# A graph network kernel on one core: one chunk's convolution a step later, a weight product in another bank, a re-ordered tail

## The chip, the core and the metric

The kernel runs on one core of one Trainium2 chip. That core has a matrix engine (TensorE, PE in the rows below, with PEld for its weight loads), a vector engine (VectorE, DVE), a scalar engine (ScalarE, ACT), GpSimd (POOL), a queue engine that only issues transfers here (SyncE, SP) and 16 DMA engines. The engines run side by side and wait for each other by semaphores. The metric is device microseconds (us) of one launch. Three runs of the kernel before gave 517.07, 517.53 and 518.02 us; the median is 517.53 us.

## The reference

The input is a batch of 16 graphs of 512 nodes with 128 features, `x`, and dense adjacency matrices `adj` of 512 x 512. Two networks follow one another, each with a residual sum and a layer norm:

```python
# 1: gated graph network, 5 layers, on every graph
A = (adj != 0)
h = x
for l in range(5):
    m   = einsum('bnd,de->bne', h, weight[l])
    agg = einsum('bij,bid->bjd', A, m)
    gi, gh = agg @ w_ih.T + b_ih, h @ w_hh.T + b_hh      # three gates each
    r, z = sigmoid(i_r + h_r), sigmoid(i_z + h_z)
    h = (1 - z) * tanh(i_n + r * h_n) + z * h
x = layernorm(x + h * nodemask)

# 2: group convolutions on nodes 0..24 of every graph, 5 groups of nodes
for g, idx in enumerate(GROUPS):
    N_g = D^-1/2 (adj[idx, idx] + I) D^-1/2
    h1  = relu(N_g @ (x[idx] @ W1[g]) + b1[g])           # 128 -> 256
    o   = relu(N_g @ (h1 @ W2[g]) + b2[g])               # 256 -> 128
    fused[idx] += softmax(fusion_w)[g] * o
out = layernorm(x + fused)
```

Everything is float32 on the outside.

## The kernel before

**Recurrence.** A step is one layer of one graph; 16 graphs and 5 layers give `K` = 80 steps, in the fixed order `GRAPH` (made from the table `ROUNDS`). A state lies transposed (feature on the partition) in float32 (`H`) and as two float16 halves (`HT`, high and low). In step k the matrix engine does, in this order: `aggregate(k + 1)`, 8 matmuls of the *next* step's messages with the adjacency matrix (fp8) into one of two banks `pA2`; `gates_of_state(k)`, three float16 products each into `pHN`, `pR` and `pZ`; `gates_of_messages(k)`, three each added into `pR` and `pZ` and written into `pIN`. The products into `pIN` wait for `h_v` = k, the end of step k-1's new state, because the engines work out the new state inside `pIN`. ScalarE reads the gates through sigmoid and tanh and makes the high halves (`aggregated_hi`, `state_hi`, `reset_gate`, `update_gate`, `new_gate`); VectorE does the low halves, the candidate and the new state (`aggregated_lo`, `candidate`, `new_state`, `state_lo`); GpSimd multiplies z and h (`kept_share`). A state goes back to node order for `aggregate` by a transposing transfer that SyncE issues two steps ahead.

**First layer norm.** After a graph's last step, `masked` (times the mask), `residual` (GpSimd), `stats_of_rows` and `variances` (VectorE), `inverse_root` (GpSimd), `scales` (VectorE: the shift `NB` for ScalarE, and for the first 32 nodes the normalised rows `X1`, semaphore `f_nb`) and `normalise` (ScalarE) follow, some steps apart; then SyncE stores the graph (`store_y`). Graphs 10 and later come back through `back`, four matrix transposes.

**Convolution.** Nodes 0 to 31 of four graphs make one chunk, four chunks in all. A chunk passes through seven stages on the matrix engine, all through the bank `pC`: A (`conv_a`: X1 with the normalised adjacency `BD`), B twice (`conv_b`: W1, one half of the 256 each), S twice (`conv_s`: W2), D twice (`conv_d`: `BD` again). ScalarE reads A, B and S, VectorE adds the biases and reads D, and `fused` sums the groups with a ReLU. The table `CONV_AT` says in which step each stage of chunks 0 to 2 is put, with 0 for "ahead of the aggregation" and 1 for "between the gates". `conv_a(c)` waits for `f_nb` = 4(c + 1), the scales of the chunk's four graphs. Graph 7, the last of the second chunk, has its last step at 47 and its `scales` on VectorE in step 53.

**Start and tail.** Before step 0 the weights are transposed and `merge(0)` multiplies layer 0's weight with the input gates' weights into `pA2[:, 1]`, where VectorE has just read the other weights (`wh_lo`). In the last two steps (78 and 79) the last chunk is worked out early in small tiles (`early_...`, tile `X` from `pA`), and after step 79 its stages B, S and D run in the banks of `LAST_BANKS`, beside the layer norms of graphs 12 to 15. S and D are split there as group 0 and groups 1 to 4. The biases are put into the bank first by a product with the identity (`biases`).

The order of every engine's work is the order of the code of its block; there is no scheduler. Each engine waits at the head of its own queue.

Of the kernel before, what the change touches and what calls it, by code (L numbers as in the profile page):

```python
# [6 lines left out]
ALU = mybir.AluOpType  # L7
# [8 lines left out]
B, N, D = 16, 512, 128  # L16
L = 5
NI = N // P
K = B * L
# [60 lines left out]
           [(54, 0), (55, 0), (56, 0), (57, 0), (58, 0), (60, 0), (61, 1)],  # L80
# [34 lines left out]
def graph_net_kernel(nc, x, adj, nodemask, weight, w_ih, w_hh, b_ih, b_hh, W1, b1, W2, b2, fusion_w, out):  # L115
    ctx = ExitStack()
    with ctx:
# [113 lines left out]
        LAST_BANKS = [pA2[:, 1, :], pC, pA2[:, 0, :], pA2[:, 1, :], pC, pA2[:, 0, :], pC]  # L231
# [79 lines left out]
        f_dn = sem("f_dn")  # L311

# [29 lines left out]
        def _(sp):  # L342
# [36 lines left out]
            def store_y(b):  # L379
                sp.wait_ge(f_on, b + 1)  # L380
                if b == B - 1:
                    sp.wait_ge(f_dn, 1)
# [46 lines left out]
        def _(pool):  # L429
# [191 lines left out]
        def _(pe):  # L621
# [206 lines left out]
            pe.wait_ge(wi_v, 1)  # L828
            pe.wait_ge(wh_lo, 1)
            merge(0, pA2[:, 1, :])  # L830
# [4 lines left out]
            pe.wait_ge(wc_lo, 1)  # L835
# [44 lines left out]
        @block.scalar  # L880
        def _(act):
# [154 lines left out]
            merged_hi(0, pA2[:, 1, :])  # L1036
# [10 lines left out]
            for k in range(1, K):  # L1047
# [25 lines left out]
                if k == EARLY + 1:  # L1073
                    read_a(TAIL, LAST_BANKS[0])
                    read_b(TAIL, 0, LAST_BANKS[1])
# [4 lines left out]
                if k >= EARLY - 1:  # L1080
                    masked(E0 + k - EARLY + 1)
                new_gate(k)
# [7 lines left out]

            act.wait_ge(c_mm, STAGES * TAIL + 4)
            fn(S2[:, 0, :], LAST_BANKS[4][:, 0:D], ACT.Copy).then_inc(c_ea, 1)
            normalise(B - 4)
            act.wait_ge(c_mm, STAGES * TAIL + 5)
            fn(S2[:, 1:G, :].rearrange("p g e -> p (g e)"), LAST_BANKS[3][:, :], ACT.Copy).then_inc(c_ea, 1)
# [5 lines left out]
        def _(dve):  # L1101
# [138 lines left out]

            def softmax_shift():
# [63 lines left out]
            def fused(c, groups):  # L1305

                first = 0 if c == TAIL else 1
                for g in groups:
# [4 lines left out]
                    else:  # L1313
                        dve.wait_ge(c_mm, STAGES * TAIL + (7 if g else 6))
# [47 lines left out]
            for k in range(1, K):  # L1362
# [16 lines left out]
                if k == EARLY:  # L1379
                    early_stats()  # L1380
                    early_x()
# [86 lines left out]
```

## Time and profile before

| what | value |
| --- | --- |
| median of 3 timed runs | 517.53 us |
| the profiled execution: its time / its span | 518.59 us / 516.8 us |
| PE busy | 496.4 us, 96% of the span |
| DVE busy | 420.5 us, 81% |
| ACT busy | 300.9 us, 58% |
| POOL busy | 223.8 us, 43% |
| mean granted TensorE clock | 0.988 |
| chain that ended last, by engine | PE 73%, DVE 17%, ACT 5%, issue 3% |

Times of the trace count from the start of the span, and busy shares are averages over the whole of it. The matrix engine is busy in 96% of it, so what matters is where it is not, and where its granted clock is under 1.00 (full speed, 2.4 GHz; 0.50 is 1.2 GHz). A float32 matmul is shown as two instructions, and a matmul's duration in a row is longer than the distance to the next one, since they are pipelined.

### The profile page before, as it was taken

The page shows a single profiled execution, that of the slowest core. Times are in us where ns is not written, and L with a number is a line of the kernel's source. Part 1 is how long each engine was busy: PE and PEld are TensorE (multiplying, and loading weights), DVE is VectorE, ACT ScalarE, POOL GpSimd, SP SyncE. Part 2 cuts the span into 40 slices and gives each one's busy share as a digit, 9 for nine tenths or more (in the row PEclk, how much of TensorE's full clock was granted, in tenths as well). Part 3 has the DMA queues.
Part 4 walks back from the last instruction along what each step waited for, and adds up shares of the span by engine and source line. Part 5 has one row for each costly group of instructions (what it writes and reads, how often), then busy time and mean ns, then how long its engine had stood idle before and what let it go on. Part 6 is the DMA issues. An engine that isn't in the chain of part 4 may idle for free.

```text
span 516.8 us, 7332 instructions
## 1 busy us (share of the span) xinstructions
PE 496.4 (96%) x2393; PEld 242.3 (47%) x2393; DVE 420.5 (81%) x799; ACT 300.9 (58%) x551; POOL 223.8 (43%) x208
## 2 busy tenths in 40 slices
PE   7899999999999999999999999699999999999985
PEld 5344444444444444444555443245454444564554
DVE  3788988899978899998778999946778988757885
ACT  4546556645555566666667655455566556755564
POOL 3533552534553466633545344524212534212464
PEclk9999999999999999999999999989999999999997
DMA  8676253655527456446725655422234242322212
GB/s 278 207 164 168 43 161 85 157 152 105 123 42 183 107 98 163 104 84 157 157 81 126 167 123 140 62 51 51 41 72 91 47 92 56 60 61 46 64 41 82
DMA packets 131611, 55.46 MB, mean 107 GB/s; under 512 B 95140, under 2 KB 123252, under 8 KB 131572
## 3 DMA queue, kind: packets, MB, share of 16 engines
q1 hardware_dynamic: 106336, 31.93, 30.6%
q10 hardware_dynamic: 25236, 23.05, 14.7%
q8 instruction: 19, 0.31, 0.2%
q14 instruction: 20, 0.16, 0.1%
HBM read 27.70 MB, written 4.19 MB: 62 GB/s over the span
## 4 chain that ended last, share of the span: by engine, by line
PE 73%; DVE 17%; ACT 5%; issue 3%; DMA 1%; POOL 1%; ACTq 0%; POOLq 0%; DVEq 0%
PE pA L652 21%; PE pR L659 5%; PE pR L657 5%; PE pR L658 5%; PE pZ L658 5%; PE pZ L657 5%; PE pZ L659 5%; PE pHN L657 3%; DVE T L1140 3%; PE pHN L658 3%; PE pHN L659 3%; PE pIN L657 3%; PE pIN L659 3%; PE pIN L658 3%; DVE H L1153 2%
## 5 line engine op out<-in xcount | busy, mean ns | idle before, releaser
L469 POOL TENSOR_TENSOR ZH<-Z,H 128x512 f32<-128x512 f32 x80 | 102.8, 1284 | 233.9 <-ACT Z L959 230.0
L652 PE MATMUL pA<-A,NAT 128*128 128x512 fp8e4 x640 | 152.9, 382 | 1.4 <-DVE A L1129 1.4
L963 ACT ACTIVATE pIN<-T,COLS 128x512 f32<-128x512 f32 x80 | 55.4, 692 | 85.1 <-DVE T L1144 85.1
L652 PEld LDWEIGHTS pA<-A,NAT 128*128 128x128 f16 x640 | 62.9, 99 | 74.6 <-issue 3.7
L946 ACT ACTIVATE HT<-H 128x512 f16<-128x512 f32 x74 | 46.7, 631 | 63.0 <-DVE H L1153 63.0
L1140 DVE SCALAR_TENSOR_TENSOR T<-pHN,BHN,R 128x512 f32<-128x512 f32 x80 | 59.7, 747 | 22.2 <-ACT R L952 22.2
L1149 DVE SCALAR_TENSOR_TENSOR pIN<-Z,pIN 128x512 f32<-128x512 f32 x80 | 55.1, 689 | 19.7 <-ACT pIN L963 19.4
L952 ACT ACTIVATE R<-pR,BRZ 128x512 f32<-128x512 f32 x80 | 54.5, 681 | 23.3 <-PE pR L659 23.3
L1158 DVE TENSOR_TENSOR HT<-H,HT 128x512 f16<-128x512 f32 x74 | 52.7, 713 | 18.7 <-ACT HT L946 13.3
L1135 DVE TENSOR_TENSOR AG<-pA,AG 128x512 f16<-128x512 f32 x80 | 54.7, 684 | 12.6 <-ACT AG L942 12.5
L942 ACT ACTIVATE AG<-pA 128x512 f16<-128x512 f32 x80 | 47.2, 589 | 24.4 <-PE pA L652 21.7
L1144 DVE TENSOR_TENSOR T<-pIN,T 128x512 f32<-128x512 f32 x80 | 55.3, 691 | 2.7
L1153 DVE TENSOR_TENSOR H<-ZH,pIN 128x512 f32<-128x512 f32 x80 | 54.9, 687 | 2.8
L959 ACT ACTIVATE Z<-pZ,BRZ 128x512 f32<-128x512 f32 x80 | 54.8, 685 | 0.0
L657 PE MATMUL pIN<-AG,WC 128*128 128x512 f16 x80 | 30.4, 380 | 1.5 <-DVE H L1153 1.4
L657 PE MATMUL pHN<-HT,WH 128*128 128x512 f16 x80 | 30.6, 383 | 1.0 <-DVE T L1140 0.6
L657 PE MATMUL pR<-AG,WC 128*128 128x512 f16 x80 | 30.3, 379 | 0.8 <-DVE AG L1135 0.8
L658 PE MATMUL pHN<-HT,WH 128*128 128x512 f16 x80 | 30.5, 381 | 0.0
L659 PE MATMUL pHN<-HT,WH 128*128 128x512 f16 x80 | 30.3, 379 | 0.0
L657 PE MATMUL pR<-HT,WH 128*128 128x512 f16 x80 | 30.3, 379 | 0.0
L658 PE MATMUL pR<-HT,WH 128*128 128x512 f16 x80 | 30.3, 379 | 0.0
L659 PE MATMUL pR<-HT,WH 128*128 128x512 f16 x80 | 30.3, 379 | 0.0
(213 smaller groups left out, 837.3 us busy)
## 6 DMA issues: line engine op xcount, KB each, us to landing
AS<-in_adj_dram ACTq DMA_DIRECT2D x13, 1024.0 KB, 6.0
XR<-in_x_dram ACTq DMA_DIRECT2D x16, 256.0 KB, 2.9
XS<-in_x_dram ACTq DMA_DIRECT2D x13, 256.0 KB, 3.2
out_dram<-Y SPq DMA_DIRECT2D x16, 192.0 KB, 2.2
AS<-in_adj_dram SPq DMA_DIRECT2D x2, 1024.0 KB, 9.7
AS<-in_adj_dram SPq DMA_DIRECT2D x4, 256.0 KB, 5.0
NAT<-HT SPq DMA_TRANSPOSE x64, 3.1
XS<-in_x_dram SPq DMA_DIRECT2D x3, 256.0 KB, 7.8
```

What stands on the lines that cost most here:

```text
L469: g_.tensor_tensor(ZH[:, :], Z[:, :], H[:, b, :], ALU.mult).then_inc(zh_p, 1)
L652: last = mm(pA2[:, k % 2, :], NAT[:, k % 2, h, i, :], A8[:, b, i, :], start=(h == 0 and i == 0), stop=(h == 1 and i == NI - 1))
L657: mm(bank[:, :], w_hi, v_hi, start=start, stop=False)
L658: mm(bank[:, :], w_hi, v_lo, start=False, stop=False)
L659: return mm(bank[:, :], w_lo, v_hi, start=False, stop=stop)
L959: fn(Z[:, :], pZ[:, :], ACT.Sigmoid, bias=BRZ[:, 1:2], scale=UNSCALE).then_inc(sig_z, 1)
L963: fn(pIN[:, :], T[:, :], ACT.Tanh, bias=BI[:, 2:3], scale=UNSCALE).then_inc(n_a, 1)
L1135: v.tensor_tensor(AG[:, k % 2, 1, :], pA2[:, k % 2, :], AG[:, k % 2, 0, :], ALU.subtract).then_inc(ag_lo, 1)
L1140: v.scalar_tensor_tensor(out=T[:, :], in0=pHN[:, :], scalar=BHN[:, 0:1], in1=R[:, :], op0=ALU.add, op1=ALU.mult).then_inc(t_v, 1)
L1144: v.tensor_tensor(T[:, :], pIN[:, :], T[:, :], ALU.add).then_inc(u_v, 1)
L1149: v.scalar_tensor_tensor(out=pIN[:, :], in0=Z[:, :], scalar=1.0, in1=pIN[:, :], op0=ALU.subtract, op1=ALU.mult).then_inc(e_v, 1)
L1153: v.tensor_tensor(H[:, GRAPH[k], :], ZH[:, :], pIN[:, :], ALU.subtract).then_inc(h_v, 1)
```

## The change

Four things are changed.

1. In `CONV_AT` the first five stages of the second chunk move one step later: 54, 55, 56, 57, 58 become 55, 56, 57, 58, 59. The last two (60 and 61) stay, and so does everything that VectorE, GpSimd and SyncE do for the chunk.
2. `merge(0)` goes into `pIN` instead of `pA2[:, 1]`, and ahead of the wait for `wh_lo`. A second wait for `wc_lo` ahead of `aggregate(1)` goes.
3. In the tail, stages S and D are split into groups 0 to 2 and groups 3 and 4. The biases are put into `pR` and `pZ` ahead of stage S, right after the last gates have been read. The first part of S stands ahead of `back(15)`, the second behind it.
4. Around it, work of the last layer norms changes engines and places. `masked(15)` goes from VectorE to ScalarE, `masked(14)` the other way. Half of graph 12 is normalised by GpSimd, and half of graph 15 by VectorE instead of GpSimd. ScalarE reads the first half of stage B after the two sigmoids of step 79. On VectorE graph 12's statistics move up into step 78, `scales(14)` stands behind the statistics of graph 15, and `fused` runs in two parts around them.

```diff
-           [(54, 0), (55, 0), (56, 0), (57, 0), (58, 0), (60, 0), (61, 1)],
+           [(55, 0), (56, 0), (57, 0), (58, 0), (59, 0), (60, 0), (61, 1)],
...
-        LAST_BANKS = [pA2[:, 1, :], pC, pA2[:, 0, :], pA2[:, 1, :], pC, pA2[:, 0, :], pC]
+        LAST_BANKS = [pA2[:, 1, :], pC, pA2[:, 0, :], pC, pA2[:, 1, :], pR, pZ]
+        LAST_PARTS = [slice(0, 3), slice(3, G)]
...
 # GpSimd, end
             residual(B - 2)
+            normalise(E0, range(2))
             residual(B - 1)
             inverse_root(B - 2)
             inverse_root(B - 1)
-            normalise(B - 1, range(2))
             inverse_root_z(TAIL)
...
 # TensorE, start
             pe.wait_ge(wi_v, 1)
+            merge(0, pIN)
             pe.wait_ge(wh_lo, 1)
-            merge(0, pA2[:, 1, :])
             gates_of_state(0, first_messages)
...
-            pe.wait_ge(wc_lo, 1)
             aggregate(1)
...
 # TensorE, end
             conv_b(1, LAST_BANKS[2])
+            pe.wait_ge(sig_r, K)
+            biases(LAST_PARTS[0], LAST_BANKS[5][:, 0:3 * D])
+            pe.wait_ge(sig_z, K)
+            biases(LAST_PARTS[1], LAST_BANKS[6][:, 0:2 * D])
             pe.wait_ge(c_ea, 5 * TAIL + 3)
+            conv_s(range(0, 3), LAST_BANKS[3])
             back(B - 1)
-            conv_s([0], LAST_BANKS[4])
-            conv_s(range(1, G), LAST_BANKS[3])
-            biases(slice(1, G), LAST_BANKS[5][:, :])
+            conv_s(range(3, G), LAST_BANKS[4])
             pe.wait_ge(c_ea, 5 * TAIL + 4)
-            biases(slice(0, 1), LAST_BANKS[6][:, 0:D])
-            conv_d(TAIL, [0], LAST_BANKS[6], True)
+            conv_d(TAIL, range(0, 3), LAST_BANKS[5], True)
             pe.wait_ge(c_ea, 5 * TAIL + 5)
-            conv_d(TAIL, range(1, G), LAST_BANKS[5], True)
+            conv_d(TAIL, range(3, G), LAST_BANKS[6], True)
...
 # VectorE, end (after step 79)
+            masked(B - 2)
             new_state(K - 1)
-            dve.wait_ge(f_mv, B - 2)
-            stats_of_rows(B - 2)
-            masked(B - 1)
-            variances(B - 2)
             scales(B - 4)
             scales(B - 3)
+            stats(B - 2)
+            fused(TAIL, range(0, 3))
             stats(B - 1)
             scales(B - 2)
+            fused(TAIL, range(3, G))
+            stats_z(TAIL)
             scales(B - 1)
-            fused(TAIL, [0])
-            fused(TAIL, range(1, G))
-            stats_z(TAIL)
+            normalise(B - 1, range(2))
             normalise_z(TAIL)
```

The table moves the stages on TensorE and ScalarE. On TensorE, around steps 53 and 54, the two matmuls of `conv_a` (`pC<-BD,X`) stand between the last gate product of step 53 (`pIN<-AG,WC`) and the aggregation of step 55 (`pA<-A,NAT`). Before:

```order
L658 MATMUL pIN<-AG,WC 128x512
L659 MATMUL pIN<-AG,WC 128x512
L755 MATMUL pC<-BD,X 128x128
L756 MATMUL pC<-BD,X 128x256
L652 MATMUL pA<-A,NAT 128x512 x8
L657 MATMUL pHN<-HT,WH 128x512
```

In the changed kernel the place after step 53 holds no convolution. The same two matmuls stand one step later, behind the `pIN` products of step 54 and ahead of the aggregation of step 56:

```order
L662 MATMUL pIN<-AG,WC 128x512
L663 MATMUL pIN<-AG,WC 128x512
L759 MATMUL pC<-BD,X 128x128
L760 MATMUL pC<-BD,X 128x256
L656 MATMUL pA<-A,NAT 128x512 x8
L661 MATMUL pHN<-HT,WH 128x512
```

So 8 aggregation matmuls, 9 products of `gates_of_state(54)` and 9 of `gates_of_messages(54)` now run before `conv_a`.

On ScalarE, from step 79's candidate to the end of the program (`pIN<-T` is the tanh, `H<-pA` the second half of stage B, `S` stage S, `YM` is `masked`, `Y` is `normalise`), before:

```order
L969 ACTIVATE YM<-pF,COLS 128x128 x4
L963 ACTIVATE pIN<-T,COLS 128x512
L1001 ACTIVATE H<-pA,COLS 128x128
L1001 ACTIVATE H<-pA,COLS 128x4x16 x4
L1092 ACTIVATE S<-pC 128x128
L988 ACTIVATE Y<-Y,NB,RS 128x128 x4
L1095 ACTIVATE S<-pA 128x512
L988 ACTIVATE Y<-Y,NB,RS 128x128 x10
```

and now:

```order
L968 ACTIVATE pIN<-T,COLS 128x512
L1006 ACTIVATE H<-pA,COLS 128x128
L1006 ACTIVATE H<-pA,COLS 128x4x16 x4
L993 ACTIVATE Y<-Y,NB,RS 128x128 x2
L974 ACTIVATE YM<-pHN,COLS 128x128 x4
L1101 ACTIVATE S<-pC 128x384
L1101 ACTIVATE S<-pA 128x256
L993 ACTIVATE Y<-Y,NB,RS 128x128 x10
```

`masked(15)` (`YM<-pHN`) now stands ahead of both reads of stage S, and the ten blocks of graphs 13, 14 and 15 are still the last work of this engine.

On VectorE the end of the program (`ST`, `MV` and `VE` are a graph's statistics, `NB` is `scales`, `FU` is `fused`, `ZO` the last chunk's result), before:

```order
L1210 BN_STATS ST<-Y 128x6 x4
L1217 BN_AGGR MV<-ST 128x2 x4
L1220 TENSOR_SCALAR VE<-MV 128x4
L1221 TENSOR_SCALAR VE<-MV 128x1
L1232 SCALAR_TENSOR_TENSOR NB<-MV,RS 128x4 x2
L1318 SCALAR_TENSOR_TENSOR FU<-pC,X 128x128
L1318 SCALAR_TENSOR_TENSOR FU<-pA,FU 128x128 x4
L1331 BN_STATS ZST<-FU 128x6
L1333 BN_AGGR MV<-ZST 128x2
L1335 TENSOR_SCALAR VE<-MV 128x1
L1341 TENSOR_SCALAR ZO<-FU,MV,RS 128x128
```

and now:

```order
L1333 SCALAR_TENSOR_TENSOR FU<-pR,X 128x128
L1333 SCALAR_TENSOR_TENSOR FU<-pR,FU 128x128 x2
L1217 BN_STATS ST<-Y 128x6 x4
L1224 BN_AGGR MV<-ST 128x2 x4
L1227 TENSOR_SCALAR VE<-MV 128x4
L1228 TENSOR_SCALAR VE<-MV 128x1
L1239 SCALAR_TENSOR_TENSOR NB<-MV,RS 128x4
L1333 SCALAR_TENSOR_TENSOR FU<-pZ,FU 128x128 x2
L1346 BN_STATS ZST<-FU 128x6
L1348 BN_AGGR MV<-ZST 128x2
L1350 TENSOR_SCALAR VE<-MV 128x1
L1239 SCALAR_TENSOR_TENSOR NB<-MV,RS 128x4
```

Three of the five `fused` operations moved ahead of the statistics of graph 15, and `scales(14)` (the first `NB`) stands behind those statistics. Two blocks of `normalise(15)` and `ZO` follow the last row shown.

## Rows read from the trace of the kernel before

**Rows 1.** TensorE's timeline, steps 53 to 56: start, us, instruction, [idle before <-releaser].
```profile
330.53 0.38 PE L659 MATMUL pIN<-AG,WC 128*128 128x512 f16 x1
334.99 0.77 PE L755 MATMUL pC<-BD,X 128*128 128x128 f32 x2 [4.08 <-DVE X L1237]
...
344.06 1.23 PE L761 MATMUL pC<-YT,W1S 128*128 128x128 f32 x10
```

**Rows 2.** Stretches there: length, busy PE, PEld, DVE, ACT, POOL, granted clock, DMA, GB/s.
```profile
334.00:336.00 2.00, 1.01 (x4) 0.95 (x5) 1.95 (x4) 0.00 (x0) 0.47 (x1) 0.50 0.00 0
...
340.00:342.00 2.00, 2.00 (x10) 0.84 (x8) 0.69 (x1) 1.94 (x5) 0.75 (x1) 0.87 0.00 0
```

**Rows 3.** Timeline of VectorE and GpSimd ahead of the convolution's first matmul.
```profile
332.87 1.59 POOL L459 TENSOR_TENSOR H<-HT 128x512 f32<-128x512 f16 x1
333.39 1.10 DVE L1232 SCALAR_TENSOR_TENSOR NB<-MV,RS 128x4 f32<-128x4 f32 x1
334.50 0.34 DVE L1237 TENSOR_SCALAR X<-Y,MV,RS 32x128 f32<-32x128 f32 x1
334.77 0.68 DVE L1149 SCALAR_TENSOR_TENSOR pIN<-Z,pIN 128x512 f32<-128x512 f32 x1
335.48 0.69 DVE L1153 TENSOR_TENSOR H<-ZH,pIN 128x512 f32<-128x512 f32 x1
```

**Rows 4.** The same pair of engines at two other graphs' scales.
```profile
198.42 1.25 DVE L1237 TENSOR_SCALAR X<-Y,MV,RS 32x128 f32<-32x128 f32 x1
198.44 1.14 POOL L475 TENSOR_TENSOR YM<-Y 128x512 f32<-128x512 f16 x1
...
272.56 0.33 DVE L1237 TENSOR_SCALAR X<-Y,MV,RS 32x128 f32<-32x128 f32 x1
272.57 1.93 POOL L459 TENSOR_TENSOR H<-HT 128x512 f32<-128x512 f16 x1
```

**Rows 5.** Timeline of the start, around the first weight product.
```profile
6.80 0.60 ACT L1035 ACTIVATE BD<-pIN 128x512 f32<-128x512 f32 x1
7.12 0.55 DVE L1115 SCALAR_TENSOR_TENSOR WH<-pA,WH 128x384 f16<-128x384 f32 x1
7.82 0.88 PE L636 MATMUL pA<-BD 128*128 128x384 f32 x2 [1.06 <-DVE WH L1115]
```

**Rows 6.** TensorE's timeline: stage S of chunk 0, then the tail.
```profile
263.57 1.95 PE L768 MATMUL pC<-W2S,H 128*128 128x128 f32 x16
...
503.74 0.63 PE L737 MATMUL pHN<-IDF,H 128*128 128x128 f32 x4 [2.15 <-ACT H L1001]
504.90 3.32 PE L768 MATMUL pA<-W2S,H 128*128 128x128 f32 x16
```

**Rows 7.** Timeline of ScalarE, the tail.
```profile
500.38 1.19 ACT L969 ACTIVATE YM<-pF,COLS 128x128 f32<-128x128 f32 x4
502.13 1.17 ACT L1001 ACTIVATE H<-pA,COLS 128x128 f32<-128x128 f32 x5
508.76 3.94 ACT L988 ACTIVATE Y<-Y,NB,RS 128x128 f32<-128x128 f32 x10
```

**Rows 8.** Timeline of VectorE and GpSimd, the tail.
```profile
505.18 1.26 POOL L482 TENSOR_TENSOR Y<-YM,XR 128x512 f32<-128x512 f32 x1 [1.74 <-DVE YM L1205]
506.59 0.86 DVE L1210 BATCH_NORM_STATS2 ST<-Y 128x6 f32<-128x128 f32 x4
510.46 1.48 DVE L1318 SCALAR_TENSOR_TENSOR FU<-pA,FU 128x128 f32<-128x128 f32 x4 [0.60 <-PE pA L774]
...
513.43 0.35 DVE L1341 TENSOR_SCALAR ZO<-FU,MV,RS 128x128 f32<-128x128 f32 x1 [0.76 <-POOL RS L494]
```

**Rows 9.** SyncE's timeline, the last stores.
```profile
511.96 0.33 SPq L383 DMA_DIRECT2D out_dram<-Y  x1
512.88 0.41 SPq L383 DMA_DIRECT2D out_dram<-Y  x1
513.83 0.58 SPq L389 DMA_DIRECT2D out_dram<-ZO  x1
```

More of the change, by code:

```diff
@@ L311, in graph_net_kernel @@
         f_dn = sem("f_dn")
+        f_dv = sem("f_dv")
         c_mm = sem("c_mm")
@@ L380, in store_y @@
                 sp.wait_ge(f_on, b + 1)
+                if b == E0:
+                    sp.wait_ge(f_dn, 1)
                 if b == B - 1:
-                    sp.wait_ge(f_dn, 1)
+                    sp.wait_ge(f_dv, 1)
                 sp.dma_start(out[b, S:P, :], Y[S:P, b % 4, 0, :]).then_inc(st_y[b % 4], 16)
@@ L1035, in _ @@
             fn(WT, pIN[:, :], ACT.Copy).then_inc(wi_v, 1)
-            merged_hi(0, pA2[:, 1, :])
+            merged_hi(0, pIN)
             natural_hi(1)
@@ L1074, in _ @@
                     read_a(TAIL, LAST_BANKS[0])
-                    read_b(TAIL, 0, LAST_BANKS[1])
                 reset_gate(k)
@@ L1079, in _ @@
                     natural_hi(3)
-                if k >= EARLY - 1:
+                if EARLY - 1 <= k <= EARLY:
                     masked(E0 + k - EARLY + 1)
+                if k == EARLY + 1:
+                    read_b(TAIL, 0, LAST_BANKS[1])
                 new_gate(k)
@@ L1089, in _ @@
             read_b(TAIL, 1, LAST_BANKS[2])
[L1091 to L1095, printed above, removed]
+            normalise(E0, range(2, NI))
+            masked(B - 1)
+            for part, groups in enumerate(LAST_PARTS):
+                act.wait_ge(c_mm, STAGES * TAIL + 4 + part)
+                n = (groups.stop - groups.start) * D
+                fn(S2[:, groups, :].rearrange("p g e -> p (g e)"), LAST_BANKS[3 + part][:, 0:n],
+                   ACT.Copy).then_inc(c_ea, 1)
             normalise(B - 3)
@@ L1239, in scales, with normalise @@
                                 ALU.subtract, ALU.mult).then_inc(f_nb, 1)
+            def normalise(b, blocks):
+                w = b % 4
+                for i in blocks:
+                    last = v.tensor_scalar(Y[:, w, i, :], Y[:, w, i, :], MV[:, w, i, 0:1], RS[:, w, i:i + 1],
+                                           ALU.subtract, ALU.mult)
+                last.then_inc(f_dv, 1)
             def softmax_shift():
@@ L1313, in fused @@
                     else:
-                        dve.wait_ge(c_mm, STAGES * TAIL + (7 if g else 6))
-                        src = LAST_BANKS[5][:, (g - 1) * D:g * D] if g else LAST_BANKS[6][:, 0:D]
+                        part = int(g >= 3)
+                        dve.wait_ge(c_mm, STAGES * TAIL + 6 + part)
+                        src = LAST_BANKS[5 + part][:, (g - 3 * part) * D:(g - 3 * part + 1) * D]
                     if g != first:
@@ L1348, in _ @@
             cast_first(1)
-            merged_lo(0, pA2[:, 1, :])
+            merged_lo(0, pIN)
             cast_first(2)
@@ L1380, in _ @@
                     early_stats()
+                    dve.wait_ge(f_mv, E0)
+                    stats_of_rows(E0)
                     early_x()
                 if k == EARLY + 1:
-                    variances(E0)
                     stats(E0 + 1)
```

3 lines of the change are left out of this document (1 added, 2 removed).

## The prediction, written before the changed kernel had run

> **What bounds the kernel now.** I read the page's busy shares first. TensorE is busy for 496.4 us of the 516.8, so the gain to be had there is the 20.4 us in which it is not, and what a low clock costs. The waits of TensorE come next, longest first, and then its timeline at each. Three places matter. The first is a single stall in the middle of the program: the first matmul of the second chunk's convolution sits idle for 4.08 us, released by VectorE's `X` [rows 1]. The last `pIN` product before it starts at 330.53. The reader should see in the stretches that the clock falls with it: 0.50 granted from 334, and 0.87 over 340 to 342 [rows 2]. The second place is the start, where the weight product waits for `wh_lo` [rows 5]. The third is the tail, where TensorE waits 2.15 us, runs its 16 float32 passes of stage S in 3.32 us against 1.95 us elsewhere [rows 6], and other engines end the program. The profiled execution took 518.59 us, 1.8 us more than its span and 1.06 us more than the median of the timed runs. I work out differences from its span and take them off the median, 517.53 us.
>
> **The middle: the convolution one step later.** Matmuls of 512 columns follow each other every 0.215 us: from 334.99 to 344.06 [rows 1] are 9.07 us, in which the clock loses 1.01 x 0.5 + 4 x 0.5 + 2 x 0.13 = 2.77 us [rows 2]. The 6.30 us left are `conv_a`, about 0.7 us (its first pair shows 0.77 at the low clock), and 26 matmuls, 8 of the aggregation and 18 of the gates: 0.215 us each.
>
> Before: TensorE is free at 330.53 + 0.22 = 330.75, and reaches 344.06 13.31 us later. After: the head of its queue is `aggregate(55)`. Its inputs are long there (graph 13 is new at that step, its adjacency was cast and its features halved steps before). 8 + 15 matmuls bring it to 330.75 + 23 x 0.215 = 335.7, where the `pIN` products of step 54 want `h_v`, the end of VectorE's new state at 335.48 + 0.69 = 336.17 [rows 3], seen 0.1 later. So a wait of 0.55 us stays in place of the 4.08: VectorE is the late engine here, and the table hides the scales behind work, not the state. By the time `conv_a` comes up (about 337), its `X` of 334.8 is old. From there the step's order has one step of cover everywhere: ScalarE reads A in step 55, and so on to step 59, and VectorE's reading of D at 60 and 61 stays. Stage D at 60 now follows S by one step instead of two, as it does in chunk 0 (steps 40 to 45), where TensorE shows no wait. That edit is at nothing, hidden by a whole step of matmuls, and would cost a fraction of a microsecond if ScalarE were late.
>
> One cost isn't in the old trace. ScalarE used to sit behind the stalled aggregation. Now it makes the halves of graph 15's features earlier, and GpSimd's subtraction for it becomes ready as its previous operation ends, at 332.87 + 1.59 = 334.46, just when VectorE wants to begin `X` [rows 3]. In the rows the two engines hold each other up: `NB`, four elements wide, took 1.10 us and ended with GpSimd's operation. In the same race elsewhere `X` lost once (1.25 us) and won once (0.33 us, and GpSimd's operation took 1.93 us) [rows 4]. The loss would put `X`, and with it the new state and `pIN`, 0.8 us later (the wait is 1.35 us). The ends are 0.55 and 1.35 us; the two rows say one each, and I take 0.95. Gain: 13.31 - 6.30 - 0.95 = 6.06 us, say 6.0 (5.65 to 6.45).
>
> The Trainium skill, page "SBUF — State Buffer", section "Who interferes with whom", says that whichever of the two engines issues first has the shared ports for its whole instruction and the other blocks fully, by order of issue and not by shape. By that rule GpSimd's operation, ready at 334.46 against `X` at 334.50, would win and the gain would be 5.65 us; by the row at 272.56 it would be 6.45 us.
>
> **The start.** The first weight product waits for VectorE's `WH` (7.12 + 0.55 = 7.67, seen at 7.82). Its new gate is ScalarE's copy, over at 6.80 + 0.60 = 7.40 [rows 5], seen at 7.5. So it starts 0.3 us earlier. The next products still want `wh_lo` at 7.8, but the 0.7 us product covers that. VectorE's casts stay where they are and are needed 2 us later. All that follows up to step 3 is a chain through all engines, which moves along. Bounds: 0 (a transfer decides instead) and 0.35. I take 0.3. The dropped `wc_lo` wait is worth nothing, since the gates just ahead have already waited for it.
>
> **The tail, on the old axis.** ScalarE now reads half a stage B instead of doing `masked(14)` (1.19 us [rows 7]) ahead of the tanh. But the candidate behind it waits for the `pIN` products anyway, so the second half of B ends at about 503.15 instead of 502.13 + 1.17 = 503.30. TensorE has spent its idle time on the biases, so it waits about 0.5 us instead of 2.15, and I expect full clock. Then: first part of S, 12 passes at 1.95/16 = 0.12 or a little less, to 504.6; `back(15)` to 505.2 with its latency; `masked(15)` on ScalarE (as the 1.19 us row) to 506.35, where VectorE had it at 505.1; the residual, 1.26 us [rows 8], to 507.65. ScalarE reads S meanwhile to 506.7, three groups of D end at 507.6, and three `fused` at 0.37 us (1.48/4 [rows 8]) end at 508.8. Only then come the statistics of graph 15 (0.86 us for the first part, 1.5 in all), to 510.25, then the scales of graph **14**. ScalarE needs them for graph 14: 4 of its 10 blocks at 3.94/10 = 0.39 us [rows 7], to 511.95, where the old kernel stood at the same time, since its SyncE issued that store at 511.96 [rows 9]. SyncE then needs 0.92 us for this graph's two transfers and 0.95 for the next one's [rows 9], and issues the last result at 513.9 against 513.83. The last result itself is ready at 513.2 against 513.43 + 0.35 = 513.78 [rows 8]; that gain of 0.6 us waits behind SyncE. Net: 0.1 us slower. Bounds: -0.6, if the scales of graph 14 come early enough for SyncE to be free, and +1.3, if TensorE stays at the low clock for its 20 passes of S (20 x 3.32/16 - 20 x 1.95/16 = 1.7 us, part of it off the path).
>
> **Sum.** 517.53 - 0.3 - 6.0 + 0.1 = 511.3 us. Of the ends, all good together give 517.53 - 0.35 - 6.45 - 0.6 = 510.1, and all bad 517.53 - 0 - 5.65 + 1.3 = 513.2.
>
> **Rivals.**
> - *The tail gains.* If `scales(14)` ends 0.6 us or more before my 510.3, SyncE is free earlier and the result's own chain decides: 517.53 - 0.3 - 6.0 - 0.6 = 510.6 us. For it: that chain has 0.6 us in hand and TensorE's idle time is used. Against it: four engines stand in a row ahead of those scales.
> - *The clock falls all the same.* The waits left in the middle (0.95 us) or in the tail (0.5 and 1 us) may be enough. In the middle this leaves half the 2.77 us or all of it: 513.9 at worst; in the tail +1.3: 512.6 us. Against it: other waits of 0.6 to 1.3 us in this trace leave 1.00; the drop at 334 had more than 3 us of idle time behind it. On the page "TensorE: Matmul & The Clock Gate", section "What's actually happening", the Trainium skill says that the throttled state is the default and only activity releases it; by that rule, too, less idle time cannot make the clock worse.
> - *The stall only moves.* If `pIN` of step 54 waited as long as `conv_a` did, the gain would be the start's: 517.2 us. The state at 336.17 speaks against it.
> - *Slower.* If `aggregate(55)` could not run at 330.75 because its features or the transfer behind them were late, TensorE would stand until the state of step 53 is through, 336.3, 1.3 us later than 334.99, and at the low clock for as long: 517.53 - 0.3 + 1.3 + 0.1 = 518.6 us. It decides from about 6 us of lateness on; the halves of graph 13 were finished 7 us ahead, so I give it little.
>
> **How the numbers follow.** The forecast 0.70, the tail's gain 0.12, the clock 0.11, the moved stall 0.04, slower 0.03. A measurement of this kernel tells about 0.2% (1 us) from no change. The first three are all faster: 0.93. The moved stall is within it: 0.04. The last is slower: 0.03. The range goes from 509.9 us, just under all the good ends, to 513.1 us, into the clock's case.
>
> **What would show it.** In the changed profile TensorE should show no wait ahead of `pC<-BD,X` at steps 54 to 56, a wait of 0.5 to 1.4 us at `pIN` of step 54 on VectorE's `H`, and a granted clock of 1.00 through 325 to 345. The first weight product should start at about 7.5. The tail, from the last `pIN` product on, should take as long as before within 0.5 us, with stage S at full speed, VectorE waiting ahead of `FU`, and SyncE's last three issues 0.9 us apart. I am wrong in the step, and not only in size, if the middle gains under 5 us, or if the tail shifts by over 1 us.

## The result, and the profile after

| | before | after |
| --- | --- | --- |
| median | 518.06 us (6 runs, 517.07 to 520.29) | 512.75 us (6 runs, 512.35 to 513.36) |
| profiled execution: time / span | 518.59 / 516.8 us | 512.55 / 510.7 us |
| mean granted clock | 0.988 | 0.993 |

The ratio after/before is 0.989, with an interval of 0.9865 to 0.9915: 1.1% faster. The forecast was 511.3 us in a range of 509.9 to 513.1, so the time lies in the range, 1.45 us above the forecast.

The page after shows TensorE 4.3 us less busy, though it runs the same matmuls. Matmuls at the low clock count longer as busy, in the middle and in stage S of the tail [rows 6]. The slice in the middle that had a low clock is gone:

```profile
PE 492.1 (96%) x2393; PEld 239.4 (47%) x2393; DVE 421.7 (83%) x801; ACT 300.3 (59%) x549; POOL 224.0 (44%) x208
...
PEclk9999999999999999999999999999999999999997
```

To see where 6.1 us of span went I cut both traces at the same pieces of work: VectorE's first operation, the aggregation that stands in one row of 16 matmuls near 29 us, the last chunk's `conv_a` (`pA<-BD,X`) and SyncE's last issue. The last two columns say what a kernel that holds one part alone gave (experiments below). Each figure comes from one profiled launch.

| stretch | before | after | difference | one part alone |
| --- | --- | --- | --- | --- |
| span's start to VectorE's first operation | 6.52 | 6.33 | -0.19 | launch, not the change |
| to the aggregation near 29 us | 23.14 | 22.76 | -0.38 | -0.38 (start) |
| to the last chunk's `conv_a` | 464.60 | 458.94 | -5.66 | -5.66 (middle) |
| to SyncE's last issue | 19.57 | 19.77 | +0.20 | +0.18 (tail) |
| to the end of the span | 2.97 | 2.90 | -0.07 | |
| span | 516.8 | 510.7 | -6.1 | |

**The middle.** TensorE's timeline of the changed kernel, the answer to [rows 1]:

```profile
330.18 1.89 PE L656 MATMUL pA<-A,NAT 128*128 128x512 fp8e4 x8
...
334.93 0.38 PE L663 MATMUL pZ<-AG,WC 128*128 128x512 f16 x1
336.49 0.39 PE L661 MATMUL pIN<-AG,WC 128*128 128x512 f16 x1 [1.19 <-DVE H L1160]
...
337.15 0.39 PE L759 MATMUL pC<-BD,X 128*128 128x128 f32 x2
...
343.42 1.22 PE L765 MATMUL pC<-YT,W1S 128*128 128x128 f32 x10
```

`conv_a` no longer waits. What is left is a wait ahead of the `pIN` products of step 54, on the new state. Counted as the prediction counted, from the last matmul's start plus 0.22, it is 336.49 - 335.14 = 1.35 us, where `conv_a` stood for 334.99 - 330.75 = 4.24 us. The stretches, with the columns of [rows 2], show the full clock right through it:

```profile
334.00:338.00 4.00, 2.81 (x15) 1.40 (x13) 3.65 (x6) 2.85 (x7) 1.03 (x1) 1.00 0.35 68
338.00:342.00 4.00, 4.00 (x20) 1.85 (x19) 3.17 (x6) 2.05 (x4) 2.38 (x2) 1.00 0.63 121
```

So 4.24 - 1.35 = 2.89 us are idle time that went, and the 2.77 us of [rows 2] are the clock in this launch of before: 5.66 together, the whole of the difference. The pair of engines of [rows 3], VectorE first, then GpSimd:

```profile
332.83 1.11 DVE L1239 SCALAR_TENSOR_TENSOR NB<-MV,RS 128x4 f32<-128x4 f32 x1
333.96 1.16 DVE L1244 TENSOR_SCALAR X<-Y,MV,RS 32x128 f32<-32x128 f32 x1
335.04 0.68 DVE L1156 SCALAR_TENSOR_TENSOR pIN<-Z,pIN 128x512 f32<-128x512 f32 x1
335.75 0.69 DVE L1160 TENSOR_TENSOR H<-ZH,pIN 128x512 f32<-128x512 f32 x1
...
332.32 1.61 POOL L463 TENSOR_TENSOR H<-HT 128x512 f32<-128x512 f16 x1
333.88 1.16 POOL L453 TENSOR_TENSOR NAT<-XS,NAT 128x512 f16<-128x512 f32 x1
```

`X` took 1.16 us instead of 0.34: it began 0.08 us after GpSimd's subtraction (`NAT<-XS,NAT`) and ended with it (335.12 and 335.04). The new state behind it is 0.8 us later.

**The start.** The weight product follows ScalarE's copy directly, the answer to [rows 5]:

```profile
6.57 0.60 ACT L1040 ACTIVATE BD<-pIN 128x512 f32<-128x512 f32 x1
7.22 0.91 PE L640 MATMUL pIN<-BD 128*128 128x384 f32 x2 [0.79 <-ACT BD L1040]
```

**The tail.** TensorE, the answer to [rows 6], with the row at which the tail begins:

```profile
488.03 0.46 PE L759 MATMUL pA<-BD,X 128*128 128x128 f32 x2
...
496.99 1.60 PE L772 MATMUL pC<-W2S,H 128*128 128x128 f32 x12 [0.49 <-ACT H L1006]
...
498.87 1.06 PE L772 MATMUL pA<-W2S,H 128*128 128x128 f32 x8
```

Twelve passes of stage S took 1.60 us where [rows 6] had 16 in 3.32. The wait ahead of them is 0.49 us instead of 2.15. ScalarE, VectorE and GpSimd, the answers to [rows 7] and [rows 8], in this order:

```profile
499.07 1.14 ACT L974 ACTIVATE YM<-pHN,COLS 128x128 f32<-128x128 f32 x4 [0.80 <-PE pHN L741]
...
504.26 2.41 ACT L993 ACTIVATE Y<-Y,NB,RS 128x128 f32<-128x128 f32 x6 [1.87 <-DVE NB L1239]
...
501.62 0.29 DVE L1333 SCALAR_TENSOR_TENSOR FU<-pR,X 128x128 f32<-128x128 f32 x1 [2.55 <-PE pR L778]
...
502.62 0.86 DVE L1217 BATCH_NORM_STATS2 ST<-Y 128x6 f32<-128x128 f32 x4
...
504.07 0.15 DVE L1239 SCALAR_TENSOR_TENSOR NB<-MV,RS 128x4 f32<-128x4 f32 x1
...
506.32 0.35 DVE L1356 TENSOR_SCALAR ZO<-FU,MV,RS 128x128 f32<-128x128 f32 x1
...
500.30 1.27 POOL L486 TENSOR_TENSOR Y<-YM,XR 128x512 f32<-128x512 f32 x1 [1.25 <-ACT YM L974]
```

Read from the bottom: graph 15's residual is there at 501.57, VectorE is just then held by the `fused` of the first three groups, begins the statistics at 502.62, and only after them comes the shift `NB` of graph **14** at 504.07, for which ScalarE has waited 1.87 us. SyncE's answer to [rows 9]:

```profile
505.93 0.33 SPq L387 DMA_DIRECT2D out_dram<-Y  x1
...
506.85 0.41 SPq L387 DMA_DIRECT2D out_dram<-Y  x1
...
507.80 0.58 SPq L393 DMA_DIRECT2D out_dram<-ZO  x1
```

The last result is ready at 506.32 + 0.35 = 506.67, 18.64 us into the tail against 19.52 before, and stands 1.13 us behind two graphs' stores.

### The profile page after: what moved, and what is told of

Read it like the earlier page. It is cut to its first block, busy times and chain, and to the rows that moved or that the text cites. A ratio compares the mean times of both kernels' runs of the same rounds, so it can differ in the third digit from the quotient of the medians.

```text
span 510.7 us, 7332 instructions
## 1 busy us (share of the span) xinstructions
PE 492.1 (96%) x2393; PEld 239.4 (47%) x2393; DVE 421.7 (83%) x801; ACT 300.3 (59%) x549; POOL 224.0 (44%) x208
## 4 chain that ended last, share of the span: by engine, by line
PE 73%; DVE 17%; ACT 5%; issue 3%; DMA 1%; ACTq 0%; DVEq 0%
PE pA L656 21%; PE pR L663 5%; PE pR L661 5%; PE pR L662 5%; PE pZ L662 5%; PE pZ L661 5%; PE pZ L663 5%; PE pIN L661 3%; DVE T L1147 3%; PE pHN L661 3%; PE pIN L663 3%; PE pHN L662 3%; PE pHN L663 3%; PE pIN L662 3%; DVE T L1151 2%
## 5 line engine op out<-in xcount | busy, mean ns | idle before, releaser
L656 PE MATMUL pA<-A,NAT 128*128 128x512 fp8e4 x640 | 151.2, 379 | 1.4 <-DVE A L1136 1.4
```

What stands on the lines that cost most here:

```text
L656: last = mm(pA2[:, k % 2, :], NAT[:, k % 2, h, i, :], A8[:, b, i, :], start=(h == 0 and i == 0), stop=(h == 1 and i == NI - 1))
```

## The experiments

The times and ratios below compare each kernel with the kernel before, run in the same job. Effects under 1 us between two changed kernels are read from one profiled launch of each, and the medians bear them out only where the text says so.

The theory after the result: the middle gives nearly all of it, half as idle time and half as clock; 0.8 us of the possible gain went to the two engines that hold each other up; the tail gives nothing, because the stores of graphs 14 and 15 decide and their order on VectorE did not improve. Its rivals: start or tail carry a part of the gain; the low clock is not caused by the idle time; `X` was slow for another reason than GpSimd's operation; the last result's own chain decides the end. "Segments" are the stretches of the table above.

### The parts one by one

**middle_only**, on the kernel before:

```diff
-           [(54, 0), (55, 0), (56, 0), (57, 0), (58, 0), (60, 0), (61, 1)],
+           [(55, 0), (56, 0), (57, 0), (58, 0), (59, 0), (60, 0), (61, 1)],
```

> The kernel before with the second chunk's first five stages one step later, and nothing else. Theory (the 4.08 us stall and its low clock go, a wait on the state of step 53 stays): conv_a without a wait, a wait of 1.2 us ahead of the pIN products of step 54, X at about 1.1 us since GpSimd's subtraction wins the race, clock 1.00 through the middle, the middle 5.7 us shorter, about 512.4 us. Rival (the gain was made by the start and the tail as well, 1 us or more): the trace of this kernel ends 4.7 us or less before that of before.

Measured: 512.69 us (4 runs) against 517.84 (21 runs), ratio 0.9906 [0.9883, 0.9928]. The medians differ by 5.15 us. The middle segment is 458.94, that of the full change to the hundredth; the wait at `pIN` is 1.19 us and `X` takes 1.16 us, as expected. The one line of the table is the change, as far as timed runs can tell. (That two launches agree so well is not a rule: see after_again.)

**start_only**, on the kernel before:

```diff
             pe.wait_ge(wi_v, 1)
+            merge(0, pIN)
             pe.wait_ge(wh_lo, 1)
-            merge(0, pA2[:, 1, :])
...
-            pe.wait_ge(wc_lo, 1)
             aggregate(1)
```

> The kernel before with the first weight product in the new gate's bank and ahead of the wait for wh_lo, and nothing else. Theory: the product starts 0.3 to 0.4 us earlier and all later work moves by just that; the changed kernel's 0.57 us at step 1 held 0.2 us of something else, the first transposes, which differ from launch to launch. Rival: the bank itself makes the first transposes faster, so this kernel too starts 0.57 us earlier. Time: 0.3 to 0.6 us less than before, too little to be told by the timed runs alone.

Measured: 517.63 us (10 runs) against 517.84, ratio 0.9998 [0.9983, 1.0013]. The medians differ by 0.21 us, where 0.3 to 0.6 was expected, and the interval reaches past 1, so the timed runs don't show a gain. The start's segment is 22.76 against 23.14, 0.38 us, but not all of that is the change. Counted from VectorE's first operation, the last transpose ahead of the weight product already starts 0.14 us earlier in this launch; 0.24 us are left. In the eight profiles of kernels that have the new start together with other changes the same segment goes from 22.76 to 23.38 us. In scales_late (23.38) the transposes run late, `WH` is over at 7.49 and ScalarE's copy only at 7.80, so the old wait would have cost nothing there. The profile of tail_only bears that out: it has the old order and late transposes, and its weight product is released by ScalarE's copy too. So the gain is there only in launches whose transposes are early. The rival, that the new bank makes the transposes faster, is out: in scales_late they are slow with the new bank. The other 0.19 us of the 0.57 by which the changed kernel was ahead at 29 us belong to its launch too.

**tail_only**, on the kernel before: the third and fourth part of the change, that is the new `LAST_BANKS` and `LAST_PARTS`, and all ends of the engines' blocks as in the diff.

```diff
-        LAST_BANKS = [pA2[:, 1, :], pC, pA2[:, 0, :], pA2[:, 1, :], pC, pA2[:, 0, :], pC]
+        LAST_BANKS = [pA2[:, 1, :], pC, pA2[:, 0, :], pC, pA2[:, 1, :], pR, pZ]
+        LAST_PARTS = [slice(0, 3), slice(3, G)]
```

> The kernel before with the new tail alone (steps 78 and 79 and what follows). Theory: stage S at full clock (12 passes 1.6 us), the second part's reading and the statistics of graph 15 ahead of the scales of graph 14, so SyncE's last three issues stand where they stood: from the last pIN product to the last issue 13.9 us against 13.7, time within 0.3 us of before. Rival (the new tail is worth its TensorE time, 1.5 us): 516 us.

Measured: 518.53 us (10 runs) against 517.84, ratio 1.0013 [0.9997, 1.003]; the tail's segment is 19.75 against 19.57. The rival that the tail gains is out. The medians differ by 0.69 us, more than the 0.3 expected, with an interval that includes the segments' 0.18.

The old tail is not the same in every launch either. In the profile of middle_only, which has it, TensorE waits the same 2.15 us as in [rows 6], and stage S runs at full speed behind it:

```profile
497.99 0.63 PE L737 MATMUL pHN<-IDF,H 128*128 128x128 f32 x4 [2.15 <-ACT H L1001]
...
498.90 1.95 PE L768 MATMUL pA<-W2S,H 128*128 128x128 f32 x16
```

The sixteen passes take 1.95 us in place of 3.32, and the tail's segment 19.46 us in place of 19.57. busy_wait has 1.95 and 19.46 too, start_only 3.28 and 19.58. So the low clock of stage S cost 0.11 us at the end of the program, and that it takes the new tail to remove it is not so. It is low in the two profiles that have the stall in the middle and full in the two that don't; whether that is more than chance, two of each don't show. Against 19.46 the new tail costs 0.31 us.

The profile of tail_only also shows two things that are not the change's, told further down.

### Idle time and clock

**busy_wait** leaves the table as it was and gives TensorE 18 matmuls that nobody reads while it waits for `X`:

```diff
+            def keep_busy(n):
+                pe.wait_ge(c_u, 2)
+                flat = WC[:, 0, :, :, :].rearrange("p h g d -> p (h g d)")
+                for _ in range(n):
+                    mm(pC[:, :], WH[:, 0, 0, :], flat[:, 0:N], start=True, stop=True)
...
+                if c == 1:
+                    keep_busy(18)
```

> The kernel before with 18 extra matmuls of 512 columns (float16, into the free bank pC, overwritten by the next product) in the stall ahead of the second chunk's conv_a. They fill 3.9 of its 4.08 us and change nothing else. Theory (the low clock cost 2.77 us on its own): granted clock 1.00 from 330 to 342 and the program 2.7 to 2.8 us faster than before. Rival (the low clock cost little, since VectorE's state of step 53 would have bound TensorE until 336 anyway): under 1.5 us faster.

Measured: 515.69 us (6 runs) against 517.84, ratio 0.9964 [0.9948, 0.9979]. TensorE's timeline of this kernel, and its stretches:

```profile
330.16 4.05 PE L744 MATMUL pC<-WC,WH 128*128 128x512 f16 x18
334.42 0.46 PE L763 MATMUL pC<-BD,X 128*128 128x128 f32 x2 [0.21 <-DVE X L1245]
```

```profile
334.00:338.00 4.00, 3.79 (x19) 1.94 (x19) 1.85 (x4) 0.93 (x2) 0.00 (x0) 1.00 0.00 0
338.00:342.00 4.00, 4.00 (x25) 2.48 (x24) 1.75 (x4) 3.76 (x9) 1.25 (x2) 1.00 0.44 64
```

`conv_a` starts 4.26 us after TensorE came free, as late as in [rows 1], and yet the clock stays at 1.00 and the middle segment is 461.90, 2.70 us shorter. The 2.77 us worked out from [rows 2] were right to 0.07, and they hang on the idle time: matmuls without any use bring them back, and all three profiles that have the stall (before, start_only, tail_only) show a low clock behind it. What is left of the 5.66 us, 2.96, is idle time. The medians differ by 2.15 us, less than the 2.7 to 2.8 expected; launches of before differ in this very term, as shown further down.

### The two engines at `X`

**port_free**, on the changed kernel: GpSimd's subtraction goes behind its `kept_share(54)`.

```diff
-                if k + 3 < K and LAYER[k + 3] == 0:
+                if k + 3 < K and LAYER[k + 3] == 0 and k != 54:
                     natural_lo(k + 3)
...
                 kept_share(k)
+                if k == 54:
+                    natural_lo(k + 3)
```

> The changed kernel with one GpSimd operation, the subtraction that makes the low half of graph 15's features, put behind the product of z and h of step 54 instead of ahead of it. So GpSimd has nothing ready when VectorE begins X at 334. Theory (X took 1.16 us because GpSimd's operation had just started): X takes 0.34 us, the state of step 53 and the pIN products of step 54 come 0.8 us earlier, the wait ahead of them falls from 1.19 to about 0.4 us. Rival (X is slow for another reason): X stays at 1.1 us and nothing moves.

Measured: 512.27 us (4 runs) against 517.46 (7 runs), ratio 0.9898 [0.9879, 0.9916]. VectorE's row, then TensorE's:

```profile
334.27 0.34 DVE L1246 TENSOR_SCALAR X<-Y,MV,RS 32x128 f32<-32x128 f32 x1
...
335.99 0.39 PE L663 MATMUL pIN<-AG,WC 128*128 128x512 f16 x1 [0.36 <-DVE H L1162]
```

The same instruction on the same data takes 0.34 us instead of 1.16, the wait at `pIN` 0.36 instead of 1.19, and the segment is 458.12, 0.82 us shorter. The slow `X` was GpSimd's doing.

**scales_late**, on the changed kernel: `scales(7)` stands behind the new state of step 53 instead of ahead of it, `normalise(7)` a step later.

```diff
                     aggregated_lo(k + 1)
+                if k == FINAL[7] + SCALED[7] + 1:
+                    scales(7)
...
-                    if k == FINAL[b] + SCALED[b] and b < E0:
+                    if k == FINAL[b] + SCALED[b] and b < E0 and b != 7:
                         scales(b)
```

> The changed kernel with the scales of graph 7 behind the new state of step 53 and the low half of step 55's messages on VectorE, and its normalise one step later on ScalarE. Theory (VectorE's NB and X, 2.2 us, stood between the candidate and the state): the wait of 1.19 us ahead of pIN of step 54 goes, conv_a still finds X ready or waits under 0.3 us, the program is 1.0 to 1.2 us faster than the changed kernel. Rival (it turns into a wait elsewhere, at conv_a or at pHN of step 55): the gain is under 0.5 us.

Measured: 511.82 us (4 runs) against 517.46, ratio 0.9888 [0.9873, 0.9903]. VectorE, then TensorE:

```profile
335.36 0.31 DVE L1239 SCALAR_TENSOR_TENSOR NB<-MV,RS 128x4 f32<-128x4 f32 x1
335.68 0.34 DVE L1244 TENSOR_SCALAR X<-Y,MV,RS 32x128 f32<-32x128 f32 x1
...
336.40 0.38 PE L759 MATMUL pC<-BD,X 128*128 128x128 f32 x2
```

TensorE waits nowhere between 333 and 338. GpSimd's subtraction now runs from 334.49 to 335.65; `NB` begins near its end and is over with it, 0.31 us instead of 1.11, and `X` comes after it at its own 0.34. The segment is 457.56, 1.38 us shorter; I had expected 1.0 to 1.2, since I counted the wait in brackets (1.19) and not the 1.35 from the end of the matmul before. The changed kernel was not timed in this job; against its 512.75 of the first comparison the median is 0.9 us lower, that of port_free 0.5.

### The tail

**scales14_first**, on the changed kernel:

```diff
             fused(TAIL, range(0, 3))
-            stats(B - 1)
             scales(B - 2)
+            stats(B - 1)
             fused(TAIL, range(3, G))
```

> The changed kernel with the scales of graph 14 ahead of the statistics of graph 15 on VectorE. Theory (ScalarE's and SyncE's last work hung on these scales): graph 14 is normalised 1.4 us earlier and stored 1.4 us earlier, but the store of graph 15 then waits for its own normalise at 506.5, so the last issue comes 0.2 us earlier. Rival (SyncE's issue time is not what decides): nothing moves, since the last result was ready at 506.7 in either case.

Measured: 512.78 us (4 runs) against 517.46, ratio 0.9915 [0.9892, 0.9937]. ScalarE and SyncE:

```profile
502.93 1.65 ACT L993 ACTIVATE Y<-Y,NB,RS 128x128 f32<-128x128 f32 x4 [0.56 <-DVE NB L1239]
505.89 0.88 ACT L993 ACTIVATE Y<-Y,NB,RS 128x128 f32<-128x128 f32 x2 [1.32 <-DVE NB L1239]
...
504.60 0.33 SPq L387 DMA_DIRECT2D out_dram<-Y  x1
...
506.80 0.33 SPq L387 DMA_DIRECT2D out_dram<-Y  x1
...
507.65 0.58 SPq L393 DMA_DIRECT2D out_dram<-ZO  x1
```

Graph 14's store goes 1.33 us earlier (504.60 for 505.93), and the last issue only 0.15 (507.65 for 507.80), with the tail beginning at 488.03 in both; the median does not show it. The idle time has gone over to graph 15: its two blocks on ScalarE now wait 1.32 us for its scales. With one graph's store early, the other's sets the end: it is issued at 506.80, 0.05 us earlier than in the changed kernel.

**stats_first**, on the changed kernel: nothing of the convolution stands ahead of graph 15's statistics.

```diff
             stats(B - 2)
-            fused(TAIL, range(0, 3))
             stats(B - 1)
             scales(B - 2)
+            fused(TAIL, range(0, 3))
             fused(TAIL, range(3, G))
-            stats_z(TAIL)
             scales(B - 1)
+            stats_z(TAIL)
```

> The changed kernel with VectorE's order in the tail turned: the statistics of graph 15 and the scales of graph 14 ahead of all five fused, and the scales of graph 15 ahead of the last chunk's statistics. Theory (in the changed kernel the first three fused wait 2.55 us for stage D and then hold up the statistics of graph 15, whose input is ready just then, by 1.0 us; on these hang the scales of graph 14 and so the last stores): the scales of graph 14 come 1.0 us earlier, the last issue 0.5 to 0.7 us earlier. Rival (ScalarE's ten blocks or the transfers themselves bind the end): the span's end moves by under 0.2 us.

Measured: 512.68 us (4 runs) against 517.96 (7 runs), ratio 0.9897 [0.9883, 0.9912]; the changed kernel once more in the same job (**after_again**) gave 512.99. VectorE:

```profile
502.41 0.87 DVE L1217 BATCH_NORM_STATS2 ST<-Y 128x6 f32<-128x128 f32 x4 [2.60 <-POOL Y L486]
```

The tail's segment is 19.21 against 19.77, 0.56 us shorter (0.3 between the medians), and ZO is ready at 18.89, so that the last store waits 0.32 us behind the others instead of 1.13. The operation whose input comes first, and on whose end the scales of two graphs wait, now stands first.

**all_of_it** joins scales_late and scales14_first, and ScalarE's own queue issues graph 15's store:

```diff
             normalise(B - 1, range(2, NI))
+            act.wait_ge(f_on, B)
+            act.wait_ge(f_dv, 1)
+            act.dma_start(out[B - 1, S:P, :], Y[S:P, (B - 1) % 4, 0, :]).then_inc(st_y[(B - 1) % 4], 16)
...
-            for b in range(B - 4, B):
+            for b in range(B - 4, B - 1):
                 store_y(b)
```

> The changed kernel with the late scales of graph 7, the scales of graph 14 first, and the store of graph 15 issued by ScalarE's queue beside SyncE's store of the last result. If the three theories hold: 1.1 us in the middle, and in the tail the last issue at the time the last result is ready, 0.8 to 1.1 us earlier than in the changed kernel: 1.9 to 2.2 us faster than it, about 510.7 us. If SyncE was not the bound: 1.1 us faster and no more.

Measured: 511.08 us (4 runs) against 517.46, ratio 0.9877 [0.9862, 0.9893]. SyncE's last issue and ScalarE's:

```profile
505.73 0.58 SPq L391 DMA_DIRECT2D out_dram<-ZO  x1
...
506.04 0.46 ACTq L1107 DMA_DIRECT2D out_dram<-Y  x1
```

SyncE issues `ZO` 18.86 us into the tail, 0.91 earlier than in the changed kernel. But the span is 509.4, only 1.3 shorter than 510.7, and the middle's 1.35 shorter segment is all of that. The transfers' table (queue, instruction, times, KB each, median us from issue to landing) says why:

```profile
out_dram<-Y SPq DMA_DIRECT2D x15, 192.0 KB, 2.1
...
out_dram<-Y ACTq DMA_DIRECT2D x1, 192.0 KB, 2.8
```

The last 192 KB were issued at 506.04 and landed 2.8 us later, at 508.84. The expectation of the tail in this kernel failed: an earlier issue of the small last store is worth nothing while a large one is issued after it. Whether the 2.8 us instead of 2.1 come from the second queue is not shown; it is one transfer.

**late_and_stats** joins scales_late and stats_first; **after_again** is the changed kernel, unaltered, in the same job.

> The late scales of graph 7 together with the turned order of VectorE in the tail. If both hold they add: 1.38 us in the middle and 0.5 to 0.7 us in the tail, 1.9 to 2.1 us faster than the changed kernel apart from the first 6 us of the launch. If the tail does not hold: 1.4 us.

> The changed kernel once more, to part what it gains from what launches differ in. The traces so far put its gain at 5.84 us apart from the first 6 us of the launch (0.38 in the start, 5.66 in the middle, 0.20 lost in the tail). Theory: the medians of the same job differ by 5.3 to 6.1 us, and single runs of either kernel scatter upwards by up to 3 us from the first steps. Rival (the profiled execution flatters it): under 5 us.

Measured: late_and_stats 511.38 us (4 runs), ratio 0.9875 [0.9853, 0.9896]; after_again 512.99 us (4 runs), ratio 0.9901 [0.9885, 0.9918]; before 517.96. The segments are 457.59 and 19.21, so both gains add: 1.35 + 0.56 = 1.91 us against the changed kernel's profile, 1.6 between the medians.

after_again missed its expectation: the medians of this job differ by 4.97 us, under the 5.3 to 6.1 expected and just under the 5 us that its rival named. So the profile of before does flatter the gain. Its own profile shows one reason more why launches differ: the middle segment is 459.52 us against 458.94, because TensorE waits for a transposing transfer (`NAT<-HT`, 0.40 us ahead of the aggregation at 118.57). The other profiles with this middle (after, middle_only, scales14_first, stats_first) have 458.93 or 458.94. So the gain of the middle can come out 0.6 us smaller in a launch for a reason that has nothing to do with the change. Its tail is 19.77 us again.

all_of_it and late_and_stats are the fastest kernels run, and these runs don't tell the two apart.

## Why the prediction was right, and where it was off

**The middle.** The mechanism held step by step: no wait at `conv_a`, a wait on `H` at `pIN` of step 54, full clock. The cost of the low clock, 2.77 us in that launch, was measured at 2.70 by busy_wait. The term was mis-sized by 0.3 us: I took 6.0 between 5.65 and 6.45 and it was 5.66. The step that failed is "the two rows say one each, and I take 0.95": the wait was 1.35, the loss case, and port_free shows that GpSimd's operation made it so. The Trainium skill, page "SBUF — State Buffer", section "Who interferes with whom", says that the engine whose instruction issues first has the ports and the other blocks for all of it. Here GpSimd was first by 0.08 us and `X` took 1.16 us in place of 0.34, so the trace agrees, and the loss case, 5.65 us, was the right one. It was in part luck that it could be worked out: the forecast had the two 0.04 us apart (334.46 and 334.50), and in [rows 4] `X` is recorded first both times, by 0.02 and 0.01 us, and yet lost once. At such distances the recorded starts do not tell who wins.

**The start.** Predicted -0.3, measured -0.38 in the trace, of which 0.14 us are the launch's. The gate is ScalarE's copy, as said. The forecast put the whole 0.3 into every launch; in those with late transposes, such as scales_late, ScalarE's copy comes last with either order.

**The tail.** Predicted +0.1, measured +0.20 (tail_only +0.18; 0.31 against the tail of middle_only). The steps came as worked out: stage S at full speed (though middle_only has that with the old tail too), VectorE idle ahead of `FU` (2.55 us), SyncE's last issues 0.92 and 0.95 us apart, the last result earlier (0.88 us against my 0.6) and stopped behind SyncE. Twelve passes took 1.60 us against my 12 x 0.12 = 1.46.

**The rivals.** *The tail gains*: its condition (scales of graph 14 earlier by 0.6 us) did not come about; stats_first and scales14_first show that the true condition was on two graphs' stores and not on one. *The clock falls all the same*: no; a wait of 1.35 us in the middle left 1.00. By the sum's own terms its worst would have been 511.3 + 2.77 = 514.1 us and not 513.9. One argument against it was also read wrongly: the clock had begun to fall before 334 (0.92 from 332 to 334), with less than 3 us of idle time behind it, and in the tail of before it fell (0.59 from 504 to 506) behind a wait of 2.15. *The stall only moves*: it moved to `pIN`, with 1.35 of 4.24 us. *Slower*: `aggregate(55)`, the row at 330.18, began without a wait.

**The 1.45 us between forecast and median.** The terms summed to -6.2 us, and the profiled spans differ by 6.1. That this agrees is in part luck: 0.19 and 0.07 us of the 6.1 lie ahead of and behind all that was changed, and the segments in between give 5.84. Of the 1.45 us, 0.5 are the base: the median of before was 517.53 in three runs and 518.06 in six. The other 0.9 are the gain, 6.2 worked out from the profile and 5.31 between the medians. The step that failed is "I work out differences from its span and take them off the median". Taken off the profiled time the sum gives 518.59 - 6.2 = 512.4, against 512.55 measured in that profile. The profiled launch of before was one in which the low clock cost much, and so was that of start_only (0.50 from 334.00 already, a middle segment of 464.58). The profile of tail_only has the same stall, and a shorter fall of the clock behind it:

```profile
338.43 0.56 PE L759 MATMUL pC<-BD,X 128*128 128x128 f32 x2 [4.08 <-DVE X L1245]
...
339.64 3.10 PE L656 MATMUL pA<-A,NAT 128*128 128x512 fp8e4 x8
```

```profile
338.00:340.00 2.00, 1.57 (x5) 1.03 (x6) 1.57 (x3) 0.00 (x0) 0.00 (x0) 0.66 0.00 0
340.00:342.00 2.00, 2.00 (x6) 0.76 (x5) 0.00 (x0) 0.00 (x0) 0.00 (x0) 0.50 0.00 0
342.00:344.00 2.00, 2.00 (x10) 0.88 (x9) 0.60 (x1) 1.23 (x3) 0.04 (x1) 0.98 0.00 0
```

Here the clock still stands at full speed when `conv_a` begins, where in [rows 2] it was at 0.50 already, and it loses 2 x 0.34 + 2 x 0.5 + 2 x 0.02 = 1.72 us instead of 2.77. The middle segment is 463.60 against 464.60: the same 1 us. So this term is not one number: it is 2.8 us in two of the three profiles that have the stall and 1.7 in the third. The timed launches of before fit it: of 21 in one job the seven at 516.99 to 517.26 us have a mean granted clock of 0.991 to 0.994, and the fourteen from 517.6 up have 0.987 to 0.990. That the fall of the clock in the middle makes all of that difference is argued, since only profiled launches show where it lies: the mean also holds the fall in stage S, which costs 0.11 us, and TensorE can wait elsewhere, as after_again shows. It would take the gain of the middle from 5.66 to between 4.6 and 5.7 us, and the medians differ by 5.15 for middle_only, 5.31 for the whole change and 4.97 in the job of after_again.

## What to carry to other kernels

A stall of the engine that does most of the work costs its own length and, where the clock falls behind it, up to two thirds of it again (1.72 to 2.77 us behind 4.24 here); look for work that is independent of what it waits for and put that first, even if the waiting work comes a whole step later. A difference worked out from one profiled execution belongs to that execution: before it is taken off a median, ask in which of its terms launches differ, and profile the unchanged kernel twice. When a last small result waits behind large stores, follow the stores back, and put first what two later operations need.

## What the runs showed of the hardware

**The clock's fall is not at a fixed place after a stall.** With the same idle time (4.08 or 4.09 us) it had fallen before the first matmul in two launches (before, start_only), and some 0.2 us into `conv_a` in another (tail_only, above). Behind the 2.15 us ahead of stage S it fell in before and start_only and stayed at 1.00 in middle_only and busy_wait. Without the idle time, in busy_wait, the middle kept 1.00.

**A launch can begin slow under a full granted clock.** In tail_only's profiled launch TensorE's first matmuls of 512 columns were 0.43 us apart, twice the usual 0.215, while the stretch reads 1.00. Its timeline and the stretch, with the columns of [rows 2]:

```profile
10.03 0.63 PE L662 MATMUL pHN<-HT,WH 128*128 128x512 f16 x1
10.45 0.63 PE L663 MATMUL pHN<-HT,WH 128*128 128x512 f16 x1
```

```profile
10.00:14.00 4.00, 4.00 (x12) 1.57 (x10) 2.64 (x6) 0.85 (x2) 1.34 (x1) 1.00 1.01 345
```

Every profiled launch begins like this: its first twelve transposes take 2.93 us under a granted clock of 1.00, and in the later ones three take 0.85 us before and 0.49 us after some point between 4.5 and 8 us. Only in tail_only it comes past 12.29. This is also why the start's segment differs by 0.6 us between launches of the same start. tail_only's is 26.45 us against 23.14, and this launch took 521.19 us where the median of its kernel is 518.53. So the granted clock in the profile does not show this case; the distance between equal matmuls does. Launches of before at 520 us may be of this sort; none of them was profiled, so that is open.

**A tiny operation can be as long as its neighbour's large one.** `NB`, four elements wide, took 1.11 us beside GpSimd's conversion (333.94 against its end at 333.93), 0.31 us in scales_late (335.67 against GpSimd's end at 335.65), and 0.15 us in the tail with GpSimd idle. Its length is the rest of the other's operation.
